# The first linear layer's input moved into the node pipeline in front of it, in a graph network on one core

## What is computed

```python
h = jnp.maximum(_layernorm(x, axis=-1), 0.0)
# L0 network: h = h @ W_enc.T + b; then twice
m = relu(concat([h[row], h[col]]) @ msg_W1[l].T + msg_b1[l]) @ msg_W2[l].T + msg_b2[l]
agg = segment_sum(m, col)
h = _layer_norm(h + concat([h, agg]) @ upd_W[l].T + upd_b[l], ln_g[l], ln_b[l])
...
x = x + (h @ W_out.T + b_out)
h = jnp.maximum(_layernorm(x, axis=-1), 0.0)      # the second normalisation
# L1 network, three times
agg = segment_sum(h[src], dst) * inv_deg
h = agg @ Wl[i].T + bl[i] + h @ Wr[i].T           # relu but after the last
x = x + h
```

## Time and profile before

| | us |
|---|---|
| median of 3 runs (3317.59 to 3323.91) | 3320.4 |
| time of the profiled execution | 3353.03 |
| its span | 3351.3 |
| last `between` stage, from its first instruction on PE to the last L1919 | 2045.7 to 2154.3 |
| input of the first linear layer, to its last L2148 on DVE | 2154.2 to 2186.1 |

### The profile page before, as it was taken

How to read it: one execution, slowest core, us unless ns; L and a number is a source line. 1 busy time by engine, 2 the same in 40 slices (tenths; PEclk the granted TensorE clock), 3 DMA queues, 4 the chain that set the end, 5 groups by cost and what they waited for, 6 DMA issues and landing times.

```text
span 3351.3 us, 219053 instructions
## 1 busy us (share of the span) xinstructions
PE 2939.6 (88%) x88775; PEld 2733.2 (82%) x88775; DVE 2504.7 (75%) x4764; ACT 2061.8 (62%) x3898; POOL 697.0 (21%) x909
## 2 busy tenths in 40 slices
PE   3666666699999998799999997799999899999999
PEld 2455555599988997699988887689999899999999
DVE  6899999777767776677767775599999855556555
ACT  1333333677767776777767775677777655555555
POOL 2221113500011115400011115344444410000000
PEclk7777777899999999899999998799999999999999
DMA  3000000566656663366656664055555488877888
GB/s 67 12 6 6 6 6 5 170 182 186 185 163 176 177 178 88 128 185 186 186 165 174 176 178 100 21 171 182 184 185 184 146 249 265 266 224 236 274 266 251
DMA packets 409150, 518.87 MB, mean 155 GB/s; under 512 B 157255, under 2 KB 280685, under 8 KB 409071
## 3 DMA queue, kind: packets, MB, share of 16 engines
q1 hardware_dynamic: 396911, 499.11, 50.3%
q0 software_dynamic: 4000, 8.20, 2.1%
q10 hardware_dynamic: 8160, 10.60, 1.1%
HBM read 408.98 MB, written 108.72 MB: 154 GB/s over the span
## 4 chain that ended last, share of the span: by engine, by line
PE 71%; DVE 12%; issue 7%; DMA 3%; ACT 3%; POOL 2%; SPq 2%; DVEq 0%; POOLq 0%; ACTq 0%
PE psum L1340 19%; PE psum L1574 17%; PE psum L1358 9%; PE psum L1344 9%; PE psum L1561 6%; PE psum L1541 3%; PE psum L698 2%; DMA cells_kept<-arena 1%; PE psum L1549 1%; DVE Hf L2135 1%; DVE Hf L936 1%; POOL arena L2048 1%; PE psum L695 1%; DVE Hf L1075 1%; DVE AGGf L981 1%
## 5 line engine op out<-in xcount | busy, mean ns | idle before, releaser
L1340 PE MATMUL psum<-tabf,arena 125*32 125x128 f16 x40256 | 1098.5, 220 | 43.4 <-issue 26.7
L1344 PE MATMUL psum<-arena 96*32 96x128 f16 x20928 | 1039.9, 221 | 10.6 <-issue 10.5
L1340 PEld LDWEIGHTS psum<-tabf,arena 125*32 125x32 f16 x40256 | 950.5, 97 | 118.5 <-issue 84.3
L1391 ACT ACTIVATE arena<-psum 128x512 f32<-128x512 f32 x1300 | 776.5, 597 | 366.6 <-PE psum L1344 314.7
L1344 PEld LDWEIGHTS psum<-arena 96*32 96x32 f16 x20928 | 700.5, 95 | 10.5 <-issue 6.9
L1574 PE MATMUL psum<-tabr,cellr 125*125 125x256 f32 x5000 | 623.7, 285 | 5.6 <-ACT cellr L1493 5.6
L1574 PEld LDWEIGHTS psum<-tabr,cellr 125*125 125x125 f32 x5000 | 606.5, 187 | 6.6 <-issue 6.6
L1358 PE MATMUL psum<-arena 128*32 128x129 f32 x10400 | 565.6, 277 | 0.4 <-issue 0.4
L1493 ACT CAST cellr<-arena 125x630 fp32r<-125x630 f16 x500 | 359.7, 720 | 268.5 <-PE psum L1574 232.4
L1493 DVE CAST cellr<-arena 125x630 fp32r<-125x630 f16 x500 | 243.9, 488 | 242.6 <-PE psum L1574 237.4
L1603 ACT CAST arena<-psum 125x500 f16<-125x500 f32 x625 | 352.8, 580 | 101.4 <-PE psum L1541 43.7
(11 more groups left out here) (312 smaller groups left out, 4451.5 us busy)
## 6 DMA issues: line engine op xcount, KB each, us to landing
arena<-cells_kept SPq DMA_DIRECT2D x500, 315.0 KB, 3.7
cells_kept<-arena SPq DMA_DIRECT2D x625, 126.0 KB
arena<-slots_turned_from SPq DMA_DIRECT2D x152, 384.0 KB, 3.4
tabf<-slots_turned_from SPq DMA_DIRECT2D x150, 384.0 KB
arena<-slots_turned_from SPq DMA_DIRECT2D x50, 512.0 KB, 3.9
tabf<-slots_turned_from SPq DMA_DIRECT2D x50, 512.0 KB
arena<-slots_turned_to SPq DMA_DIRECT2D x152, 96.0 KB, 4.1
tabf<-slots_turned_to SPq DMA_DIRECT2D x150, 96.0 KB
```

The lines of the kernel that those rows point to most:

```text
L1340: pe.matmul(psCell[b][q:q + GW, g * D:(g + 1) * D], fr, rows, start=g == 0 and p == 0, stop=False, tile_position=(0, q), skip_group_check= ...
L1344: m = pe.matmul(psCell[b][q:q + GW, g * D:(g + 1) * D], toB[part][:, here + q:here + q + GW], cur[:, part, g, :], start=g == 0 and 4 * k + ...
L1391: act.activation(msgs[:, SLOT[pos], :, 0:D], psCell[SLOT[pos]].rearrange("p (c d) -> p c d", d=D), ACT.Relu).then_inc(f_msg, 1)
```

## The change

The loops of the last `between` run on to step 42 (`INPUT_STEPS`), and from step 14 (`INPUT`) on every engine ends its step `p` with the input work of duo p-14, one step behind the second normalisation of that duo. The input stage of layer 0 as such is gone; the ones of layers 1 and 2 call the same step functions, with their banks as before. So that all results in flight have a place in PSUM, the aggregate's and the turned rows' pairs become single banks in the last `between` (banks 0 and 4), and the input of layer 0 gets one bank for its transposes (1) and one for its products (5) in place of two and four. Each reuse of a bank then waits for the duo just before. `hT` moves to words that are free in this stage. The core of the diff:

```diff
+INPUT = TABLE + 1
+INPUT_STEPS = DUOS + INPUT + 4
...
+        def own_bank(pair, l, q):
+            return pair[0 if l + 1 == L0 else q % 2]
+
         def turn_pe(pe, l, q):
             pe.wait_ge(m_n, (l + 1) * DUOS + q + 1)
-            reused(pe, m_h, l * DUOS + q - 1)
+            reused(pe, m_h, l * DUOS + q - (0 if l + 1 == L0 else 1))
...
         def between_pe(pe, l):
+            last = l + 1 == L0
             pe.wait_ge(s_agg, l + 1)
-            for p in range(-1, DUOS + MULT):
+            if last:
+                pe.wait_ge(s_lin, 1)
+            for p in range(-1, INPUT_STEPS if last else DUOS + MULT):
                 if p + 1 < DUOS:
...
-                    reused(pe, m_aTc, l * DUOS + q - 1)
+                    reused(pe, m_aTc, l * DUOS + q - (0 if last else 1))
...
+                if last and p >= INPUT:
+                    input_pe_step(pe, 0, p - INPUT)
...
         def between_act(act, l):
-            for p in range(-1, DUOS + (TABLE if last else SPLIT)):
+            for p in range(-1, INPUT_STEPS if last else DUOS + SPLIT):
...
+                if p == INPUT:
+                    act.wait_ge(l_list, 16)
+                if p >= INPUT:
+                    input_act_step(act, 0, p - INPUT)
...
         def between_dve(dve, step, l):
-            for p in range(DUOS + MULT):
+            for p in range(INPUT_STEPS if last else DUOS + MULT):
...
                     scale_dve(dve, step, x // PER, norm_at(l, 1, x // PER))
+                if p >= INPUT:
+                    input_dve_step(dve, 0, p - INPUT)
...
+        def turned_rows(l, q):
+            return psT[q % 2][:, 0:2 * D] if l else bank[1][:, 0:2 * D]
+
+        def input_pe_step(pe, l, p):
+            weights = wT[:, LIN_L + l:LIN_R + l + 1:LIN_R - LIN_L, :]
+            if p < DUOS:
+                if l == 0:
+                    pe.wait_ge(m_self, L0 * DUOS + p + 1)
+                reused(pe, p_copy, linear_at(l, p - (2 if l else 1)))
+                for w in range(2):
+                    m = pe.transpose(turned_rows(l, p)[:, w * D:w * D + P], AGG[:, 2 * p + w, 0:D], ident[0:P, 0:P])
+                m.then_inc(p_turn, 1)
+            if 1 <= p <= DUOS:
+                q = p - 1
+                pe.wait_ge(p_copy, linear_at(l, q))
+                reused(pe, p_root, linear_at(l, q - (4 if l else 1)))
+                for w in range(2):
+                    m = pe.matmul(product(l, q, w), hT[:, q % 2, w, 0:P], weights, start=True, stop=True)
+                m.then_inc(p_prod, 1)
```

More of the change, by code:

```diff
@@ L1908, in between_act @@
                     act.wait_ge(m_nT, l * DUOS + q + 1)
[L1909 removed]
+                    act.activation(HT[:, duo(q), :], own_bank(psNT, l, q)[:, 0:2 * D].rearrange("k (w p) -> k w p", w=2)[:, :, 0:P], ACT.Identity,
                                    bias=cols[:, C_B + l:C_B + l + 1], scale=cols[:, C_G + l:C_G + l + 1]).then_inc(m_h, 1)
@@ L2079, in linear_at @@
             return l * DUOS + q + 1
-        def input_pe(pe, l):
[L2083 to L2090, removed]
-            for p in range(DUOS + 1):
[L2092 to L2106, removed]
@@ new lines, in input_pe, with products, product, input_act_step @@
+        def input_pe(pe, l):
+            pe.wait_ge(s_agg, L0 + l)
+            for p in range(DUOS + 1):
+                input_pe_step(pe, l, p)
+        def products(l, q):
+            return (psO[q % 4] if l else bank[5])[0:P, :].rearrange("p (t n d) -> p t n d", t=2, n=2)
+        def product(l, q, w):
+            return products(l, q)[:, w]
+        def input_act_step(act, l, p):
+            if p < DUOS:
+                act.wait_ge(p_turn, linear_at(l, p))
+                reused(act, p_prod, linear_at(l, p - 2))
+                act.activation(hT[:, p % 2, :, 0:P], turned_rows(l, p).rearrange("k (w p) -> k w p", w=2)[:, :, 0:P], ACT.Relu).then_inc(p_copy, 1)
+            q = p - 2
+            if 0 <= q < DUOS:
+                act.wait_ge(p_rows, linear_at(l, q))
+                act.copy((TABR if l else TABL)[:, duo(q), 0, :], H[:, duo(q), :]).then_inc(m_hi, 1)
+            q = p - 4
+            if 0 <= q < DUOS and q % PER == PER - 1:
+                act.wait_ge(p_rows, linear_at(l, q))
+                store_rows(act, q // PER)
@@ L2112, in input_act @@
         def input_act(act, l):
-            if l == 0:
-                act.wait_ge(l_list, 16)
             for p in range(DUOS + 4):
[L2116 to L2129, removed]
+                input_act_step(act, l, p)
@@ new lines, in input_dve_step @@
+        def input_dve_step(dve, l, p):
+            if p < DUOS:
+                dve.wait_ge(p_prod, linear_at(l, p))
+                dve.tensor_copy(H[:, duo(p), :], products(l, p)[:, :, 0, :]).then_inc(p_rows, 1)
+                root = products(l, p)[:, :, 1, :]
+                if l == L1 - 1:
+                    if p == 0:
+                        dve.wait_ge(p_in, NB_LOOPS)
+                    dve.tensor_tensor(AGG[:, duo(p), 0:D], root, X[:, duo(p), :], ALU.add).then_inc(p_root, 1)
+                else:
+                    dve.tensor_tensor(AGG[:, duo(p), 0:D], root, bias[:, B_LIN + l:B_LIN + l + 1, :].to_broadcast([P, 2, D]), ALU.add
+                                      ).then_inc(p_root, 1)
+            q = p - 2
+            if 0 <= q < DUOS:
+                dve.wait_ge(m_hi, L0 * DUOS + linear_at(l, q))
+                table = TABR if l else TABL
+                high = TABR[:, duo(q), 0, :].bitcast(F32) if l else TABL[:, duo(q), 0, :]
+                low = dve.tensor_tensor(table[:, duo(q), 1, :], H[:, duo(q), :], high, ALU.subtract)
+                if q % PER == PER - 1:
+                    low.then_inc(s_tab, 1)
@@ L2131, in input_dve @@
         def input_dve(dve, l):
             for p in range(DUOS + 2):
[L2133 to L2150, removed]
+                input_dve_step(dve, l, p)
```

20 lines of the change are left out of this document (10 added, 10 removed).

## The result

The change made the kernel slower: median 3337.74 us (3330.87 to 3344.99, 6 runs) against 3322.15 us (3317.59 to 3325.6, 6 runs) of before, 15.6 us more, ratio 1.0048 with a 95% interval of 1.0034 to 1.0063. The profiled execution took 3344.99 us. That of before was a longer one of its kernel (3353.03) and had reached this stage 28.1 us later (2045.6 against 2017.5). So I compare the stage, not the spans: from its start to the first L1541 on PE it took 143.95 us before and takes 159.2 now, 15.3 more.

The account below looks back on a forecast made before the run. The prediction saw a serial PE-DVE-ACT chain at block ends, ACT setting the pace between them. 70.8 + 9 + 2 + 20 = 101.8 us against 92.85, so 9.0 slower (+3 to +20): 3329.4 us, range 3316 to 3343.

Parts of the forecast that it names:

- Where the cost arises: At block ends from step 14 on: DVE's sums and statistics queue behind input work, so the next root waits.
- The six windows: Root to root, steps 14 to 31, now 55.3 us: 70.8 at full clock, plus 9 for half clock, 2 for slow instructions.
- The tail: Step 31's root to the end, eight products through one bank: 17.5 us at full clock, put at 20; now 37.5.
- half-clock end: Tail with PE at half clock throughout, 2.75 us a duo: 24.7 us.
- The sign given for the tail: In the profile after, L2149 follows L2149 at 1.9 to 2.7 us and PE waits for L2156.
- the stretch near 102 us: From step 14's root to the last L2163, forecast near 102 us; now 92.85.
- Single banks of aggregate and turned rows at nothing: Last `between`: their reuse waits costed at nothing; before step 14 at most 1.4 us more.
- Full clock for PE: Rival: PE stays at full clock in most of the merged stretch, time change -4.5 to +3 us; chance 0.25.
- Half clock all along: Rival: PE at half clock throughout the merged stretch, +20 to +30 us; chance 0.08.
- The Trainium skill's rule: If it held for the whole merged stretch, the half-clock sum would be approached, a loss near 29.6 us.
- The faster rival: Input hides in the waits: six windows keep 55.3 us, tail 20, a gain of 17.5 us; chance 0.10.
- (A): The experiments' theory: DVE's input work stands before the next step's statistics and waits for a product, lengthening the six windows.

Follow-up runs that it names:

- the second kernel: The changed kernel, but DVE takes each input duo one step later (duo p-15 in step p): 3318.64 us, ratio 0.9985 to the kernel before.
- the seventh kernel: The changed kernel, but DVE puts input work off only where the next step ends a block: 3360.32 us, ratio 1.0008 to the kernel before.
- the fifth kernel: The changed kernel with DVE's input work one step later and more input banks from duo 12 on: 3343.27 us, ratio 0.9952 to the kernel before.

## Why the prediction was right, and where it was off

The forecast was 9.0 us slower, measured were 15.6, inside the range and on the predicted side. By its own steps:

- **Where the cost arises: right.** The chain that the prediction built (input copy, product, next step's product, then DVE's input work, sums, statistics, root) is the one in the timeline. That it is the order on DVE, and not the work, is shown by the second kernel, which does the same work in 18.35 us less (some 10 us of it without the clock's help). The 7.2 us that are left over the kernel before are the moved work itself and what goes with it; no run divides them.
- **The six windows: right in sum, in part by luck.** 70.8 + 9 + 2 = 81.8 forecast, 80.92 measured, as two errors cancel. The first four windows carry more than their 1.5 us for half clock and slow small instructions (10.0, 12.8, 10.0 and 12.8 became 11.78, 15.41, 12.48 and 14.80), the last two less (9.1 and 16.1 became 10.08 and 16.37). The half clock came to some 5 us a window on average and not 4, and PE did not always resume at it as the prediction has it: in the first window it resumed at full clock, which fell 0.8 us later.
- **The tail: the step that failed.** The term was put "between its ends, 20 us", because PE would wait four tenths of the time at full clock. It measured 26.48, above even the half-clock end of 24.7. In the traces the forecast was 5.55 us short (14.55 for 9.0): 6.48 in the tail, less 0.9 in the windows. The further 1.0 us up to the medians' 15.6 lies within the ratio's interval, 11 to 21 us. Two things were wrong in it. The clock was put between the two levels, and it was 0.50 throughout: 4.7 us, up to the half-clock end. And the loop's sum, 1.95 + 0.75 + 0.05 = 2.75 us, is really 2.08 + 0.76 + 0.14 = 2.98, as the hand-over and a product that starts behind a wait cost more than the earlier trace rows showed; seven of these make 1.6 us. No row stood behind the 0.05 for the hand-over. At full clock the loop is likewise 2.04 and not 1.87 (the second kernel). The sign given for the tail, L2149 every 1.9 to 2.7 us, was missed for the same reason, and the stretch near 102 us became 107.4; PE waits for L2156 as said, though most brackets name ACT's copy.
- **Single banks of aggregate and turned rows at nothing: right**, 0.3 us from root 4 to root 14 in the kernel that has them alone.
- **The rivals.** Full clock for PE fell: each of the six windows has a stretch at half clock (clocks of 0.70 to 0.90). Half clock all along held for the tail and not for the windows. The Trainium skill's rule (TensorE: Matmul & The Clock Gate, psum-queue depth-cycling), that small idle times through a queue of banks make the clock swing between its levels, is not what the changed kernel's tail does: the row shows 0.50 there without a swing. With the same banks the second kernel's tail has 0.97, and only the seventh kernel's swings once, down and up again. In the six windows the clock does swing, but there PE stands for several us at each root (up to 4.8 us at L1812 by the list of waits), which is more than a small idle time.
- **The faster rival**, that the input hides in the waits if its work is done before the statistics are due, was given 0.10 for the change as it is, and rightly did not happen. Its mechanism is real, though: one step later instead of earlier, most of the same work hides (all but 7.2 us in the six windows), and with the banks given back the stage gains 14.8 us where this rival had 17.5.

The two parts do not add up exactly, since they meet in the clock: the second kernel repairs only (A), and its tail falls by 7.7 us as well, seven times the 0.94 us between the loop's two periods and a little more. How much of the six windows' growth is half clock and how much DVE's order can't be parted cleanly for the same reason: fewer waits also went with less half clock (a mean clock of 0.89 in the second kernel, of 0.81 over the six rows of the changed one). The 8.5 us above are only an upper estimate of the clock's part.

## What to carry to other kernels

When a stage is folded into a pipeline, look at every in-order engine for what stands behind the new work: here two or three instructions, of which the first waited for a late product, stood in front of the statistics for which ACT and then PE wait, and the same work one step later made the six windows 18.35 us shorter. Sum the loop of a single-buffered bank from the start of the product to its copy, both copies and the hand-over, at both clock levels, and give the loop more banks as soon as other stages of the pipeline have drained.

## What the runs showed of the hardware

TensorE's clock has the levels 1.2 GHz (0.50 in the rows) and 2.4 GHz (1.00). The single-bank loop ran at either of them, and not at the higher one where PE was the busier. At half clock PE was busy 19.15 of 26.48 us (72%, and again on the second chip), and 60.95 of 81.76 us (75%) in the kernel with 25 such duos, and the granted clock stayed at 0.50 to the end. In the second kernel the same loop kept PE busy for only 10.45 of 18.82 us (56%), and the clock stayed at 1.00 for as long as PE worked (0.97 over the tail). The level is not kept for certain, though: in the seventh kernel the same loop fell to 0.50 at 2168.8 and was back at 1.00 at 2172.2. The two levels make a difference of 0.94 us a duo (2.98 and 2.04).

With two extra transposes a duo the clock rose to 1.00 after 6.7 us of the tail, which was 5.6 us shorter; that is one trace against three of the loop without them that stayed at 0.50, and the seventh kernel came back without any, so it is likely and not certain that the transposes did it. Denser work with three product banks went with a rise too (0.78 over the tail, 14.42 us), and with PE entering at full clock it was 1.00 and 13.35 us.

What PE did before it entered: it had stood 4.16 us in the three traces with the tail of the change (0.50 behind the wait), 3.85 us with three product banks (0.50), 2.12 and 2.02 us in the second and the fifth kernel (1.00), and 2.96 us in the seventh (1.00, and 0.50 one us later).
